# Graph network layer: node features arrive transposed, their scales come back from memory on all partitions, and layer 2 of the nodes runs on split activations

## What is computed

```python
h = jnp.maximum(_layernorm(x, axis=-1), 0.0)
...
rel_inputs = jnp.concatenate([objects[senders], objects[receivers], relations], axis=-1)
rel_effects = _mlp(rel_inputs, re_w1, re_b1, re_w2, re_b2)
agg_effects = jax.ops.segment_sum(rel_effects, receivers, num_segments=objects.shape[0])
effect_inputs = jnp.concatenate([objects, agg_effects], axis=-1)
updated_objects = _mlp(effect_inputs, ea_w1, ea_b1, ea_w2, ea_b2)
...
x = x + updated_objects
```

## Time and profile before

| | us |
|---|---|
| median of 3 runs | 969.56 (969.46 to 970.05) |
| the profiled execution | 968.67 |
| its span | 966.9 |

### The profile page before, as it was taken

One profiled execution on the slowest core, in us unless ns is written; L12 is line 12 of the kernel. 1 busy time (PEld: TensorE's weight loads), 2 busy tenths in 40 slices (PEclk: granted clock), 3 DMA queues, 4 the chain that ended last, 5 costly groups with the idle time before them and its releaser, 6 DMA issues.

```text
span 966.9 us, 20070 instructions
## 1 busy us (share of the span) xinstructions
PE 938.2 (97%) x6058; PEld 834.2 (86%) x6058; DVE 674.7 (70%) x2057; ACT 553.1 (57%) x1082; POOL 577.2 (60%) x600
## 2 busy tenths in 40 slices
PE   4879999999999999999999999999999999999997
PEld 3668988998898898899889889988988998898886
DVE  5876776777677677767767776776776677677552
ACT  1356556556655655665565666566566556655653
POOL 7777666665665666566566656656665665662220
PEclk9999999999999999999999999999999999999999
DMA  6354444454544545454454545545444544543332
GB/s 197 91 130 114 138 139 137 144 145 133 159 144 133 143 143 146 131 158 143 131 151 143 142 129 156 146 128 164 134 143 125 157 144 129 164 138 117 109 91 70
DMA packets 114100, 132.51 MB, mean 137 GB/s; under 512 B 17984, under 2 KB 70080, under 8 KB 113984
## 3 DMA queue, kind: packets, MB, share of 16 engines
q1 hardware_dynamic: 101440, 105.43, 36.3%
q0 software_dynamic: 12544, 25.72, 10.6%
HBM read 92.07 MB, written 39.00 MB: 136 GB/s over the span
## 4 chain that ended last, share of the span: by engine, by line
PE 93%; DVE 4%; issue 1%; ACT 1%; DMA 0%; POOL 0%; SPq 0%; DVEq 0%; POOLq 0%
PE l_ps L514 32%; PE l_ps L529 27%; PE l_ps L519 16%; PE agg_ps L483 9%; PE edge_ps L467 4%; PE node_ps L475 4%; PE node_ps L459 1%; DVE h L767 1%; DVE st L726 1%; DVE st L731 0%; DVE hot L807 0%; DVE lo L774 0%; DMA gath<-in_x,dst_all 0%; DMA drow_i<-in_dst_rows 0%; POOL gath L374 0%
## 5 line engine op out<-in xcount | busy, mean ns | idle before, releaser
L374 POOL DMA_INDIRECT gath<-in_x,dst_all x196 | 193.6, 988 | 59.9 <-issue 59.9
L374 POOL DMA_INDIRECT gath<-in_x,src_all x196 | 188.1, 960 | 52.2 <-issue 45.8
L780 DVE SCALAR_TENSOR_TENSOR lo<-node_ps,hi 128x512 fp32r<-128x512 f32 x98 | 67.8, 692 | 202.7 <-ACT hi L621 202.7
L397 POOL TENSOR_TENSOR ea_lo<-ea_in,ea_hi 128x512 fp32r<-128x512 f32 x45 | 63.1, 1401 | 217.0 <-ACT ea_hi L612 217.0
L529 PE MATMUL l_ps<-w2n,hid 128*128 128x128 f32 x1568 | 190.9, 275 | 0.0
L529 PEld LDWEIGHTS l_ps<-w2n,hid 128*128 128x128 f32 x1568 | 183.0, 192 | 0.1
L630 ACT ACTIVATE hid<-l_ps,b1n 128x512 f32<-128x512 f32 x196 | 135.3, 690 | 81.9 <-PE l_ps L519 81.7
L638 ACT ACTIVATE h<-xin,shift,rs 128x128 f32<-128x128 f32 x392 | 165.0, 483 | 0.0
L514 PE MATMUL l_ps<-hi,w1n_hi 128*128 128x512 f32 x392 | 155.8, 398 | 0.6 <-ACT hid L630 0.6
L514 PE MATMUL l_ps<-hi,w1n_lo 128*128 128x512 f32 x392 | 155.4, 396 | 0.0
L390 POOL TENSOR_TENSOR xb<-xin,b2n 128x512 f32<-128x512 f32 x98 | 124.5, 1292 | 33.2 <-DVE res L801 33.2
(11 more groups left out here) (94 smaller groups left out, 1441.8 us busy)
## 6 DMA issues: line engine op xcount, KB each, us to landing
win<-rel_rows SPq DMA_DIRECT2D x392, 66.0 KB
xin<-in_x_tiles SPq DMA_DIRECT2D x98, 256.0 KB, 4.1
out<-res SPq DMA_DIRECT2D x98, 256.0 KB, 3.3
rel_rows<-rel_row SPq DMA_DIRECT2D x49, 264.0 KB
ea_in<-in_ea_t SPq DMA_DIRECT2D x49, 256.0 KB, 3.1
gath<-in_x,src_all POOLq DMA_INDIRECT x196, 2.7
gath<-in_x,dst_all POOLq DMA_INDIRECT x196, 2.6
w1e<-in_L_gnn_re_w SPq DMA_DIRECT2D x1, 384.0 KB
```

The costliest lines, as they stand in the source:

```text
L374: nc.gpsimd.indirect_dma_start(gath[b][:, s, k, :], None, x, bass.IndirectOffsetOnAxis(ap=idx[:, e * T + k:e * T + k + 1], axis=0)).then_i ...
L397: nc.gpsimd.tensor_tensor(ea_lo[e % 2][:, :], ea_in[e % 2][:, :], ea_hi[e % 2][:, :].bitcast(F32), ALU.subtract).then_inc(ea_lo_set, 1)
L780: nc.vector.scalar_tensor_tensor(out=lo[r][:, 0, :], in0=node_ps[:, :], scalar=0.0, in1=hi[r][:, 0, :].bitcast(F32), op0=ALU.max, op1=ALU. ...
```

## The change

Node features are held twice in memory: `x` by rows, for gathers and statistics, and `x_t`, the transpose. For each tile `xt` is loaded with features on partitions, which removes the turn of nodes on PE and the normalisation of nodes on ACT. Statistics are still taken from rows, so scale and shift of a node lie on the partition of that node. They are now written to memory (`keep_norm`, 128 x 16 values for a pair) and read back as one row onto all 128 partitions (`load_norm`, 8 KB a partition, 1 MB a pair) one step ahead. POOL multiplies (`scale_nodes`), DVE adds the shift (`shift_nodes`), ACT and DVE split the result from SBUF.

Layer 2 of nodes now takes `w2n` as weights, split in `w2hi` and `w2lo`, and the activations as the moving side, split in `hid_hi` (ACT) and `hid_lo` (DVE for r = 1, POOL for r = 2): six products of 512 columns in place of eight float32 products of 128. Its output has features on partitions, so the bias is a column, the raw features are added from `xt`, and `out` is stored transposed. `keep_x` goes. Normalising gathered rows moves in joint steps from DVE to ACT, except the last block of each group (`last_normed`). The order of each engine within a step is written anew.

```diff
-            def keep_x(r, j, fast):
...
+            def scale_nodes(r, j):
+                pool.wait_ge(norm_loaded[j % 2], 16 * (j // 2 + 1))
+                pool.wait_ge(xt_loaded[r][j % 3], 16 * (j // 3 + 1))
+                wait(pool, node_lo_set, tile_no(r, j - 1) + 1 if j > 0 else 0)
+                nc.gpsimd.tensor_tensor(fours(h[r]), fours(xt[r][j % 3]), spread_norm[j % 2][:, :, 0, r - 1, :],
+                                        ALU.mult).then_inc(scaled[r], 1)
...
+            def keep_norm(j, fast):
+                sp.wait_ge(shift_set, stats_turn(j, fast) + 1)
...
+            def load_norm(j):
+                sp.wait_ge(norm_kept, 16 * (j + 1))
...
             def joint_step(e, j):
...
                 if e + 2 < EG:
                     load_ea(e + 2)
+                for r in (1, 2):
+                    load_xt(r, j + 1, True)
+                for r in (1, 2):
+                    load_window(r, j + 1)
+                for r in (1, 2):
+                    load_x(r, j + 3, True)
+                keep_norm(ahead, True)
                 if j > 0:
                     store(2, j - 1, True)
...
                 store_rel(e, True)
+                load_norm(ahead)
                 store(1, j, True)
...
+            def layer2_nodes(r, j, turn):
+                wait(pe, results, turn - 1)
+                for c in range(C):
+                    pe.wait_ge(hid_hi_set, C * tile_no(r, j) + c + 1)
+                    nc.tensor.matmul(l2_ps[turn % 2][:, :], w2hi[:, c, :], hid_hi[r][:, c, :], start=(c == 0), stop=False)
+                    nc.tensor.matmul(l2_ps[turn % 2][:, :], w2lo[:, c, :], hid_hi[r][:, c, :], start=False, stop=False)
+                for c in range(C):
+                    pe.wait_ge(hid_lo_set[r], C * j + c + 1)
+                    last = nc.tensor.matmul(l2_ps[turn % 2][:, :], w2hi[:, c, :], hid_lo[r][:, c, :], start=False, stop=(c == C - 1))
...
+                    if r == 0 and j == 0:
+                        sum_window(1, 0)
+                        sum_window(2, 0)
+                sum_window(1, j + 1)
+                layer2(turn)
+                layer2_nodes(1, j, turn + 1)
...
+            def shift_nodes(r, j):
+                dve.wait_ge(scaled[r], j + 1)
+                nc.vector.tensor_tensor(fours(h[r]), fours(h[r]), spread_norm[j % 2][:, :, 1, r - 1, :], ALU.add).then_inc(normed[r], 1)
...
             def node_results(r, j, fast):
                 turn = node_turn(r, j, fast)
                 dve.wait_ge(l2_done, turn + 1)
-                dve.wait_ge(xb_set[r], j + 1)
                 wait(dve, stored[r], 16 * j)
```

More of the change, by code:

```diff
@@ L94, in gnn_program @@
         end_row = sb("end_row", [P, ROW])
-        tiles = [2 * T, T, T]
         parts = [2, 2, 2]
-        h = [sb(f"h{r}", [P, tiles[r], D]) for r in range(3)]
+        h = [sb("h0", [P, 2 * T, D]), sb("h1", [P, G]), sb("h2", [P, G])]
         st = sb("st", [P, ST, 6])
@@ L552, in edge_step @@
                 layer1(0, e, turn, 1)
-                layer2(0, turn)
+                layer2(turn)
                 if e < FIRST:
@@ L680, in joint_step @@
+                hidden_nodes(1, j, turn + 1, 1)
+                deviations(e + 1, some(e + 1, EG), pair_of(e + 1))
+                high_hidden(1, j, turn + 1, 1, before_node(1, j, True))
+                hidden_nodes(2, j, turn + 2, 0)
                 if more:
-                    normalise(2, j + 1, True, range(0, 2))
-                deviations(e + 1, some(e + 1, EG), pair_of(e + 1))
-                hidden(0, turn, 1, before_edge(e, True))
+                    normalise_edges(e + 1, range(0, 1))
```

404 lines of the change are left out of this document (229 added, 175 removed).

## The result

The changed kernel takes **1067.86 us** (median of 4 runs, 1064.4 to 1076.0) against 969.51 for the kernel before: a ratio of **1.103, 95% interval 1.096 to 1.109**. I had forecast 936, faster, in a range up to 991. The sign was wrong, and the time lies outside the range. The profiled execution has a span of 1062.3 us.

A forecast was written before the change was run, and what follows sets the result against it. PE bound the kernel at 18.74 us a joint step; afterwards POOL would at 18.1. 46 x (18.74 - 18.1) = 29.4 plus 4 for both ends, off 968.67, gives 935.3; with 0.9 to the median, 936 us, range 895 to 991.

The forecast's parts named there:

- PE's own work: PE in a joint step: without node turns (0.88) and with shorter layer 2 (0.74), 18.74 falls to 17.12 us.
- ACT: ACT in a joint step: 11.4 - 0.8 + 2.6 = 13.2 us, hidden under PE's 17.12.
- The features' strided access: `shift_nodes` on DVE between 0.6 and 1.3 us, lower end taken; `scale_nodes` on POOL 1.24, if slow 1.84.
- Each on which POOL has to wait costs it 0.54: POOL's 16.5 us step grows 0.54 us per DVE pass it waits on; three of five taken, giving 18.1.
- a rival with a chance of 0.21: POOL's run of 3.7 us keeps the ports, delaying DVE and PE: mean step 19.3 us, 991 us, chance 0.21.
- The normalisations: By the skill's rule, the two edge normalisations left on DVE would join the queue for the ports shared with POOL.
- n = 4: POOL waits on four DVE passes a step: steps of 18.45 to 18.7 us, 952 to 964 us, chance 0.10.
- Whoever starts first keeps it for the whole instruction: SBUF port pair shared by DVE and POOL: the first to start holds it for one instruction, the other fully blocks.
- three meetings: Earlier rows where DVE's `hot` and POOL operations overlapped: `hot` took 1.12 and 1.91 us, `ea_lo` 1.84; said to fit the rule.
- The loop through SP: From store through windows, second `hot`, result and layer 2 to the next store: 17.3 to 18.2 us a step.
- Start: Before the first joint step: edge layer 1 comes at once, gaining 5 us, ends 2 and 6.
- wrong altogether: Sign against the whole forecast: PE waiting for `hi` of nodes, or a strided operation that takes 1.8 us.

The follow-up runs named there:

- no_low2: The changed kernel without POOL's two `hid_lo` of tile 2, PE's third products reading `hid_hi` instead: 992.4 us, ratio 1.021.
- ports: A separate kernel without graph network: DVE and POOL operations, alone and side by side; 16 two-operand DVE operations take 9.72 us alone, 18.24 beside POOL's.
- act_norm: The changed kernel with all its work, the last two edge normalisations of each joint step moved from DVE to ACT: 1047.7 us, ratio 1.081.
- no_low1: The changed kernel without DVE's two `hid_lo` of tile 1, PE's third products reading `hid_hi` instead: 1044.8 us, ratio 1.076.
- no_scale: The changed kernel without POOL's two products a step, the shift added to `xt` instead: 1052.3 us, ratio 1.084.
- no_low1_act: `no_low1` with the last two edge normalisations of each joint step moved from DVE to ACT: 1007.1 us, ratio 1.038.
- no_low12: The changed kernel without any of the four `hid_lo`, PE reading `hid_hi` instead with as many products: 962.3 us, ratio 0.993.

## Why the prediction was wrong, point by point

- **PE's own work: right.** 17.12 forecast, 17.25 in the even stretch.
- **ACT: right.** 13.2 forecast; 58.54% of a step of 20.91 is 12.2, and PE hardly waited for it.
- **The features' strided access: right.** `shift_nodes` takes 0.64 (1.28 for two), near the lower end, and `scale_nodes` 1.27.
- **"Each on which POOL has to wait costs it 0.54": the step that failed.** I had the mechanism and gave the bill to the wrong engine. POOL hardly waits inside its runs; DVE waits, for up to 4.80 us and not half a microsecond, and DVE is the engine on PE's path. The row with the truth was in the earlier trace rows: `hot` at 57.70 stood through two operations, and that pair, from 56.56, was the only one of the rows that stood directly behind a gather (which had ended at 56.54). I used it only for a rival with a chance of 0.21, on an expected 19.3 us a step. The measured 20.91 lies beyond that, and the rival had left out what stands behind the first run: POOL's two `hid_lo` (without them, in `no_low2`, the mean step is 19.40) and the late `xt` and windows of every other step or so.
- **The normalisations: the trace came out for the rule.** `ports` shows them held, 11.98 us in place of 4.19. By the Trainium skill, VectorE: DVE Perf Modes, "Mode 2×_2P", a float32 `tensor_scalar` on SBUF uses both read ports for its one tensor; the hold in `ports` agrees with that. But the prediction turned it into one more meeting for POOL, n = 4, and 952 to 964 us. It belonged on DVE's side: two of them in front of `res` cost 20 us in the whole kernel (`act_norm`) and 38 in `no_low1`.
- **"Whoever starts first keeps it for the whole instruction": too weak here.** By the Trainium skill, SBUF — State Buffer, "SBUF: two separate sides", the lock lasts for one instruction. In `ports` two streams do alternate by instruction, but a DVE operation begun 0.64 us ahead of POOL's run of three lost to all three, 4.89 us. The measurement decides. The prediction said that its three meetings agreed with the rule. The third did not: `hot` had begun at 57.70, before the second of POOL's two operations (2.50 us together from 56.56), and stood through it all the same.
- **The loop through SP: 17.3 to 18.2 forecast, 21.2 in `no_scale`** (513.00 to 534.24). The terms that were off: from store to windows 6.24, not 4.43, since the issue of edge attributes takes 1.49 and that of two `xt` 1.78, not 0.455 each; and `hot` to the next store 7.2, not 4.7, with `hid_lo` and the normalisations held. In the changed kernel `hot` waits for windows for 24.8 us in all and POOL for `xt` for 47.7; the loop is a limit beside the holds, in about half of the steps.
- **Start: the 5 us were there** (8.0 by the start of the first joint step), and the first joint step gave them back: 27.18 us against 19.55. Its shift of 16 values is held by the run of three, and `hot` and PE behind it:

```profile
70.00 4.40 DVE L838 SCALAR_TENSOR_TENSOR norm<-total,norm 128x16 f32<-128x16 f32 x1
...
75.18 2.04 PE L548 MATMUL agg_ps<-hot,win 128*128 128x128 f32 x8 [3.83 <-DVE hot L895]
```

- **What I had called "wrong altogether"**, PE waiting for `hi` of nodes, did not occur (`xt` did land late, but it was POOL that waited). `res` and `hot` late were named under "right" and "slower", and those signs are what came.

The halves say it most shortly. Against 969.5, layer 2 alone is -23 us and the features alone -2; a sum would be -25. The whole is +98. Without DVE's `hid_lo` it is 23 less, without POOL's 75 less, without both 106 less: 962.

What stays open: by which rule a single operation of DVE is held through several of POOL when two streams alternate; what a gather in front of POOL's operation has to do with it; and why the steps alternate between the two kinds. POOL's two `hid_lo` also delay its gathers and products; `no_low1_act` is still 45 us above `no_low12`, and how much of that is this delay and how much further holds was not separated.

## What to carry to other kernels

When two engines exclude each other, ask not how long an overlap lasts but which one has a run of back-to-back work: the other can lose the whole run, and whatever is next in its queue with it, however small. Put such runs where the other engine owes nothing to the bottleneck, or give the urgent operation an operand in PSUM (timed in `ports` only, not in the kernel). And two halves of a change that each cost nothing can cost 10% together, so build and time them apart: here the half without the readback was the faster kernel.

## What the runs showed of the hardware

- One two-operand operation of DVE, issued 0.34 us or more after the start of an indirect gather on POOL that has three two-operand operations behind it, took 4.3 to 4.9 us in place of 0.69. Issued 0.28 us after the gather's start or sooner, it took 0.69. The sharp edge was not expected, and the kernels have it too: directly behind a gather, 151 of 155 were held up to 0.65 us ahead of POOL's operation and none of 64 from 0.67 on; where POOL had been idle after its gather, none of 185.
- The size of the held operation does not matter: 16 values a partition (0.17 us) took 3.07 and 4.40.
- Float32 normalisations with column operands are held by POOL's operations (11.98 us in place of 4.19) and cost POOL nothing (9.80 and 9.80). Two-operand ones slow both (18.24 and 13.44). With one operand in PSUM neither loses (9.66 and 9.83).
- PE's granted clock, as a mean over a stretch, was 0.93 in one where PE was busy for 86.10 of 100 us, and 1.00 in another where it was busy for 119.99 of 142, in equal steps.
